# Router logits of the second expert layer taken from the state-space block's products, and the front of both expert layers put in another order

## The chip, the cores and the metric

The kernel runs on 1 core of a Trainium2 chip. The metric is device time in microseconds (us) of that core. Before the change three runs took 2043.24, 2030.67 and 2032.51 us, median 2032.51. TensorE is PE in the profile, VectorE is DVE, ScalarE is ACT, GpSimd is POOL; SP issues most DMAs.

## The reference, cut to what matters

Four blocks with residual sums work on 4 sequences of 1024 tokens of width 256: attention, an expert layer, a state-space block (mamba), and the same expert layer again with the same weights.

```python
x = x + attention(layernorm(x))
x = x + ffn(layernorm(x))
x = x + mamba(layernorm(x))        # its own residual adds the normed x once more
x = x + ffn(layernorm(x))

def ffn(x):                        # 4096 tokens, 4 experts, 1 taken per token
    logits = x @ Wr + br
    top_w, top_idx = top_k(softmax(logits), 1)
    h = silu(x @ Wg[e]) * (x @ Wu[e])        # 1024 wide
    return (h @ Wd[e])[top_idx] * top_w

def mamba(x):                      # returns x + ...
    z, xBC, dt = x @ w_in          # 512, 768 and 8 columns
    # convolution over 4 taps, chunked state-space product, gate by silu(z)
    y = y * rsqrt(mean(y * y) + eps) * norm_w
    return x + y @ w_out           # 512 to 256 columns
```

## The kernel before, in words

Tokens lie in 32 tiles of 128 rows, held on chip in `X` (shown as `x_res`). The four blocks run one after the other; between two of them all engines meet. Each engine runs its own list of instructions in written order and waits at semaphores.

**An expert layer** (`routed_ffn`, names `g_...`, `F["turn"]` 0 or 1) has a front and a loop of 35 slots. A slot is 128 tokens of one expert. The front makes the list of tokens for each slot:

- SP issues the loads of gate and up weights `w_gu` (8 DMAs of 1 MB, L1141), then the store of the last quarter of `X` to DRAM (`save_rows`, L106, 1 MB), on one queue.
- PE turns all 32 tiles (`turn_group`, L1476, 8 groups), ACT copies them out (L1425), PE multiplies them by the router's weights in two halves (`route`, L1490), ACT copies the logits (L1431), PE turns them back (L1499), DVE scales and shifts them (`scores`, L1206 and L1211).
- DVE finds the best expert of each token (L1219 to L1227), ranks tokens with two PE products, and works out each token's place (L1231 to L1251). Then it waits for the store (`saved`), since the marks that it writes next (L1254 on) lie where `X` was. It makes the token list `token_i` (L1274).
- POOL gathers the rows of the first slots (L1374). DVE normalises a slot's rows (`stats` L1299, `center` L1308), PE turns them (L1538), and DVE splits them into a rounded part and its remainder (`take`, L1313 and L1315).
- Weights are split in the same way, in 8 pieces of 128x2048: ACT rounds (`raise_high`, L1419), DVE subtracts (`lower`, L1183, written back over `w_gu`). The first slot's products (`first_up`, L1555) use the rounded weights first; their last part waits for all 8 remainders.
- Behind the pieces DVE works out the weights of the tokens (`weights`, L1278 to L1286). PE sorts them by slot with 32 products (`find(1, ...)`, L1524), and only after that goes on to the second slot (L1578).

The written order decides where the 8 subtractions stand: two ahead of each half of the scores (4), two behind the token list, two behind the first `take`.

**Mamba** (names `m_...`) runs for each of the 4 sequences a stage of convolutions (6 groups of 128 channels; `taps`, L1810 and L1811, three DVE operations of 128x1024 each) and then a loop over 8 tiles. `sizes` (L2184) multiplies each tile by the last 8 columns of `w_in`; `step_sizes` (L1821) takes the result. `output` (L2297) is 12 products per tile with `w_out`, split like the other weights into `w_out_hi` and `w_out_lo` (`scale_out`, `split_out`: L1801, L1802, L1914, L1916). `last` (L1905) adds the result to `X`. In the first stage POOL masks the decays (L1991).

## Time and profile before

| | us |
|---|---|
| median of three runs | 2032.51 (2030.67 to 2043.24) |
| the profiled execution's own time | 2058.66 |
| its span, first to last instruction | 2057.0 |
| attention | 0 to 795 |
| front of the first expert layer | 795 to 865 |
| its slots | 865 to 1204 |
| mamba | 1204 to 1654 |
| front of the second expert layer | 1654 to 1721 |
| its slots | 1721 to 2057 |

PE is busy 88% of the span, DVE 63%, ACT 43%, POOL 35%. A share of the span is an average over these six stages. In the two stages of slots PE is busy 327 of 336 to 339 us, in the two fronts 31 to 34 of 67 to 70 us, where DVE is busy 50 to 52 us. So a front is read from its own chain of waits and its timeline.

### The profile page before, as it was taken

How to read it: one execution, taken by the hardware profiler on the slowest of the kernel's cores; microseconds unless marked ns; L12 is line 12 of the kernel's file. 1: busy time of each engine (PE TensorE's matmuls, PEld its weight loads, DVE VectorE, ACT ScalarE, POOL GpSimd, SP SyncE). 2: the span in 40 equal slices, each digit the busy share in tenths (PEclk: the TensorE clock that was granted, in tenths of full speed). 3: DMA queues.
4: the chain of work that ended last, by engine and by line, in shares of the span. 5: the costliest groups of instructions: out<-in, count | busy, mean ns of one | idle time of the engine just before them, and what ended most of it. 6: DMA issues, size and time to landing. Idle time of an engine off the chain costs nothing. (4 is left out here: it accounts for less than half of the span.)

```text
span 2057.0 us, 32460 instructions
## 1 busy us (share of the span) xinstructions
PE 1803.7 (88%) x10701; PEld 1199.7 (58%) x10701; DVE 1290.4 (63%) x3148; ACT 877.0 (43%) x1799; POOL 724.4 (35%) x873
## 2 busy tenths in 40 slices
PE   5579989999989895499999968999899947999998
PEld 4133444444434333488888844848485736888886
DVE  4477677777676703755555528777777766555554
ACT  2146665665665743122222216474747451222221
POOL 2326355464463421123222213434343312232221
PEclk9668999999897957699999979999999978999999
DMA  5623353442544715267676642020202044676764
GB/s 157 211 80 114 113 150 108 127 129 93 152 132 143 224 53 193 94 241 258 240 257 243 240 143 83 1 103 1 103 1 103 1 186 184 239 260 238 259 244 173
DMA packets 103472, 312.39 MB, mean 152 GB/s; under 512 B 23304, under 2 KB 54796, under 8 KB 93200
## 3 DMA queue, kind: packets, MB, share of 16 engines
q1 hardware_dynamic: 84304, 257.06, 35.6%
q0 software_dynamic: 15936, 50.35, 8.1%
q10 hardware_dynamic: 3072, 2.90, 0.5%
q8 instruction: 93, 1.52, 0.3%
q14 instruction: 67, 0.55, 0.1%
HBM read 245.12 MB, written 53.87 MB: 145 GB/s over the span
## 5 line engine op out<-in xcount | busy, mean ns | idle before, releaser
L774 ACT ACTIVATE a_probs<-a_ps_e 128x512 f32<-128x512 f32 (+3 forms) x768 | 336.0, 491 | 183.3 <-PE a_ps_e L949 180.1
L511 DVE CUSTOM_DVE_ANT_0 a_ps_m<-a_ps_m,a_causal 128x512 f32<-128x512 f32 (+3 forms) x512 | 238.3, 517 | 84.1 <-PE a_ps_m L936 83.3
L1460 ACT CAST hidden_high<-g_ps_h 128x512 fp32r<-128x512 f32 x140 | 75.2, 590 | 398.8 <-PE g_ps_h L1605 398.8
L515 DVE TENSOR_REDUCE a_peak<-a_ps_m 128x1 f32<-128x512 f32 x256 | 164.1, 683 | 101.2 <-PE a_ps_m L936 99.9
L966 PE MATMUL a_ps_a<-a_probs,a_vals 128*32 128x256 f32 (+2 forms) x2560 | 216.8, 415 | 1.2 <-ACT a_probs L774 0.6
L949 PE MATMUL a_ps_e<-a_q_st,a_k_st 64*128 64x512 f32 (+3 forms) x768 | 189.6, 487 | 29.3 <-ACT a_probs L774 19.8
L653 POOL TENSOR_SCALAR_AFFINE_SELECT a_probs<-a_probs 128x256 f32<-128x256 f32 x256 | 104.5, 410 | 288.8 <-ACT a_probs L774 287.4
L936 PE MATMUL a_ps_m<-a_k_st,a_q_st 64*128 64x512 f32 (+3 forms) x768 | 157.0, 408 | 49.5 <-DMA a_k_st<-a_scr_k 23.0
L949 PEld LDWEIGHTS a_ps_e<-a_q_st,a_k_st 64*128 64x128 f32 x768 | 80.1, 204 | 199.2 <-ACT a_probs L774 137.7
L111 POOL TENSOR_TENSOR g_xe_rs<-g_xe_ve,table 128x1 f32<-128x1 f32 x70 | 39.4, 563 | 441.3 <-DVE g_xe_ve L1301 441.3
L1593 PE MATMUL g_ps_y<-g_w_d,hidden_high 128*128 128x512 f32 x560 | 144.2, 400 | 5.9 <-DVE x_res L1337 5.9
L1455 ACT ACTIVATE x_res<-g_ps_g 128x1024 f32<-128x1024 f32 x70 | 71.9, 1028 | 171.4 <-PE g_ps_g L1578 117.4
L936 PEld LDWEIGHTS a_ps_m<-a_k_st,a_q_st 64*128 64x128 f32 x768 | 86.3, 211 | 84.9 <-issue 36.7
L1321 DVE TENSOR_TENSOR x_res<-x_res,g_ps_u 128x1024 f32<-128x1024 f32 x70 | 85.5, 1222 | 69.2 <-PE g_ps_u L1578 69.2
L1593 PEld LDWEIGHTS g_ps_y<-g_w_d,hidden_high 128*128 128x128 f32 x560 | 106.2, 190 | 32.0 <-issue 6.3
L1328 DVE TENSOR_TENSOR hidden_less<-g_ps_h,hidden_high 128x512 fp32r<-128x512 f32 x140 | 90.2, 686 | 47.5 <-ACT hidden_high L1460 47.4
L1374 POOL DMA_INDIRECT x_res<-g_x_rows,g_token_i x70 | 76.0, 1086 | 93.5 <-DVE g_token_i L1274 73.1
L1313 DVE CAST g_xe_hi<-g_ps_x 128x256 fp32r<-128x256 f32 x70 | 29.8, 425 | 120.8 <-PE g_ps_x L1538 120.7
L966 PEld LDWEIGHTS a_ps_a<-a_probs,a_vals 128*32 128x32 f32 x2560 | 53.5, 114 | 81.3 <-issue 55.5
L1578 PE MATMUL g_ps_g<-g_w_hi,g_xe_hi 128*128 x272 | 91.6, 418 | 0.3 <-DVE g_xe_hi L1313 0.3
L2004 POOL TENSOR_TENSOR m_y<-m_y,m_z_act 128x512 f32<-128x512 f32 x32 | 40.7, 1272 | 135.0 <-DVE m_y L1894 119.3
L1578 PE MATMUL g_ps_u<-g_w_gu,g_xe_hi 128*128 x272 | 85.7, 396 | 0.0
(316 smaller groups left out, 3907.3 us busy)
## 6 DMA issues: line engine op xcount, KB each, us to landing
g_w_d<-down_rows SPq DMA_DIRECT2D x70, 2048.0 KB, 7.8
a_q_st<-a_scr_q POOLq DMA_DIRECT2D x32, 512.0 KB, 4.4
a_k_st<-a_scr_k POOLq DMA_DIRECT2D x32, 512.0 KB, 5.5
m_spread_acs<-m_acs_rows SPq DMA_DIRECT2D x8, 2048.0 KB, 10.0
a_scr_q<-a_high SPq DMA_DIRECT2D x34, 256.0 KB
a_scr_k<-a_high SPq DMA_DIRECT2D x32, 256.0 KB
a_swapped<-a_raw SPq DMA_DIRECT2D x64, 128.0 KB, 2.0
g_x_rows<-x_res SPq DMA_DIRECT2D x8, 1024.0 KB, 12.5
```

The lines of the kernel that those rows point to most:

```text
L511: nc.vector.tensor_tensor_reduce(ps_m[:, bank, 0:w], ps_m[:, bank, 0:w], causal[:, 512 - w:], 1.0, MASKED, ALU.add, ALU.max, peak[:, p % 2 ...
L515: nc.vector.tensor_reduce(peak[:, p % 2, r, i, c:c + 1], ps_m[:, bank, 0:w], AX, ALU.max).then_inc(chunk_max, 1)
L653: nc.gpsimd.affine_select(tile, tile, [[0, 2], [1, P]], ALU.is_ge, 0.0, base=0, channel_multiplier=-1).then_inc(masked, 1)
L774: nc.scalar.activation(probs[:, N % RING, r, q0:], ps_e[:, (2 * N + r) % HEAD_BANKS, q0:], ACT.Exp, scale=DH ** -0.5).then_inc(exp_done, 1)
L936: nc.tensor.matmul(banks[r][:, 0:w], q_st[rows(r), p % BUFS, i * P:(i + 1) * P], k_st[rows(r), p % BUFS, 512 * c:512 * c + w], start=True, ...
L949: nc.tensor.matmul(ps_e[:, (2 * N + r) % HEAD_BANKS, q0:], k_st[rows(r), p % BUFS, j * P:(j + 1) * P], q_st[rows(r), p % BUFS, 512 * c + q ...
L966: last = nc.tensor.matmul(ps_a[32 * u:32 * u + 32, some], vals[:, b % 2, j, 17 * h:17 * h + 32], probs[:, (U * CORE + 2 * m + u // 2) % RI ...
L1321: nc.vector.tensor_tensor(hid, gate, ps_u[:].rearrange("p b f -> p (b f)"), ALU.mult).then_inc(hid_ready, 1)
L1328: nc.vector.tensor_tensor(hid_lo[:, some], ps_h[:, c], hid_hi[:, some].bitcast(F32), ALU.subtract).then_inc(ht_lo, 1)
L1374: nc.gpsimd.indirect_dma_start(out=xe[:, j % XE], out_offset=None, in_=x_rows, in_offset=bass.IndirectOffsetOnAxis(ap=token_i[:, j:j + 1], ...
L1578: last = nc.tensor.matmul(ps[:, c], x[:, d * P:(d + 1) * P], w[:, :, d].rearrange("p a f -> p (a f)"), start=(n == d == 0), stop=(n == len ...
L1593: nc.tensor.matmul(ps_y[:], hid_hi[:, f * P:(f + 1) * P], w[:, f], start=(f == 0), stop=False, skip_group_check=True)
```

## The change

In mamba, 4 router columns go beside what is multiplied anyway. `sizes` gets a table `w_sizes` of 12 columns (8 step sizes, 4 router columns), loaded by two small DMAs ahead of `w_in`. Once, at the start, PE turns `w_out` (`turn_w_out`), ACT copies it, and PE multiplies it by the router's weights (`route_weights`); DVE scales and splits the 16 values of each row (`routed_columns`) into 4 new columns of `w_out_hi` and `w_out_lo`. So each product of `output` is 260 columns wide in place of 256. DVE adds the parts up in `raw_logits`: `growth` and `add_means` for each sequence, one operation in `step_sizes`, and one of 128x4 in each `last`.

In the second expert layer turning the tiles, the router's products and turning the logits back are left out; DVE reads `raw_logits` (`ready_scores`). In the first layer PE and ACT do all logits before ACT rounds the first piece of the weights. In both layers ACT rounds the 8 pieces in a row; DVE's subtractions ahead of the scores are gone. POOL does pieces 0 and 1, behind the roots of the variances and ahead of its wait for the token list; DVE does two pieces behind the token list and four behind the first `take`.

```diff
+        BY_POOL = (0, 1)
+        BY_DVE = [n for n in range(len(PIECES)) if n not in BY_POOL]
...
-            sp.wait_ge(turned_ps, HALVES)
+            if F["turn"] == 0:
+                sp.wait_ge(turned_ps, HALVES)
...
-            for n in range(2):
-                lower(n)
-            scores(0)
-            for n in range(2, 4):
-                lower(n)
-            scores(1)
+            def ready_scores():
+
+                step(nc.vector.tensor_tensor(logits[:], C["raw_logits"][:], all_experts(rstd[:]), ALU.mult))
+                step(nc.vector.tensor_tensor(logits[:], logits[:], shift[:], ALU.add))
+
+            if F["turn"] == 0:
+                scores(0)
+                scores(1)
+            else:
+                ready_scores()
...
-            for n in range(4, 6):
+            for n in BY_DVE[:2]:
                 lower(n)
             stats(0)
             center(0)
             take(0)
-            for n in range(6, len(PIECES)):
+            for n in BY_DVE[2:]:
                 lower(n)
             stats(1)
...
+            for n in BY_POOL:
+                e, d = PIECES[n]
+                pool.wait_ge(hi_ready, n + 1)
+                nc.gpsimd.tensor_tensor(columns(e)[:, d].bitcast(F32R), columns(e)[:, d], w_hi[:, e, d].bitcast(F32),
+                                        ALU.subtract).then_inc(lo_ready, 1)
             pool.wait_ge(saved, 16 * BATCH)
             pool.wait_ge(token_ready, 1)
...
-            for g in range(4):
-                turned(g)
-            raise_high(0)
-            take_logits(0)
-            turned(4)
-            raise_high(1)
-            turned(5)
-            raise_high(2)
-            turned(6)
-            turned(7)
-            raise_high(3)
-            take_logits(1)
-            for n in range(4, len(PIECES)):
+            if F["turn"] == 0:
+                for g in range(4):
+                    turned(g)
+                take_logits(0)
+                for g in range(4, 8):
+                    turned(g)
+                take_logits(1)
+            for n in range(len(PIECES)):
                 raise_high(n)
...
-            for g in range(2):
-                turn_group(g)
-            sum_weights()
-            for g in range(2, 4):
-                turn_group(g)
-            route(0)
-            turn_group(4)
-            turn_logits(0)
-            for g in range(5, 8):
-                turn_group(g)
-            route(1)
-            turn_logits(1)
+            if F["turn"] == 0:
+                for g in range(4):
+                    turn_group(g)
+                sum_weights()
+                route(0)
+                turn_group(4)
+                turn_logits(0)
+                for g in range(5, 8):
+                    turn_group(g)
+                route(1)
+                turn_logits(1)
+            else:
+                sum_weights()
...
+        SIZES = MHEADS + EXPERTS
+        sizes_ps = ps_r[:, 1, 0:T * SIZES].rearrange("p (t h) -> p t h", h=SIZES)
...
+        w_out_hi = sb("w_out_hi", [P, ZT, D + EXPERTS], F32R)
+        w_out_lo = sb("w_out_lo", [P, ZT, D + EXPERTS], F32R)
...
+                sp.dma_start(w_sizes[:, :, 0:MHEADS], M["w_in"][:, INNER + CONV:].rearrange("(t p) e -> p t e", p=P)
+                             ).then_inc(w_in_ready, 16)
+                sp.dma_start(w_sizes[:, :, MHEADS:SIZES], M["Wr"].rearrange("(t p) e -> p t e", p=P)
+                             ).then_inc(w_in_ready, 16)
             sp.dma_start(w_in[:], M["w_in"].rearrange("(t p) e -> p t e", p=P)).then_inc(w_in_ready, 16)
...
+                sp.dma_start(w_r[:], M["Wr"].rearrange("(t p) e -> p t e", p=P)).then_inc(route_in, 16)
...
+                    dve.wait_ge(w_turned, DT)
...
+                nc.vector.tensor_tensor(raw[:, b * T:(b + 1) * T], sizes_ps[:, :, MHEADS:SIZES],
+                                        grown[:].unsqueeze(2).to_broadcast([P, T, EXPERTS]), ALU.mult
+                                        ).then_inc(parts_used, 1)
+
+            def growth(b):
+
+                some = slice(b * T, (b + 1) * T)
+                if b >= 1:
+                    dve.wait_ge(rstd_ready, b + 1)
+                    dve.wait_ge(parts_used, b)
+                step(nc.vector.tensor_tensor(grown[:], var_eps[:, some], rstd[:, some], ALU.mult))
+                step(nc.vector.tensor_scalar(grown[:], grown[:], 1.0, None, ALU.add))
+
+            def add_means(b):
+
+                some, per_tile = slice(b * T, (b + 1) * T), [P, T, EXPERTS]
+                dve.wait_ge(parts_used, b + 1)
+                step(nc.vector.tensor_tensor(by_mean[:], mean_var[:, some, 0].unsqueeze(2).to_broadcast(per_tile),
+                                             w_sums[:].unsqueeze(1).to_broadcast(per_tile), ALU.mult))
+                step(nc.vector.tensor_tensor(raw[:, some], raw[:, some], by_mean[:], ALU.add))
+
+            def routed_columns():
+
+                dve.wait_ge(routed_ps, 1)
+                dve.wait_ge(loaded, 16 * 5)
+                step(nc.vector.tensor_tensor(routed[:], ps_z[:, 0, 0:ZT * EXPERTS].rearrange("p (k e) -> p k e", e=EXPERTS),
+                                             norm_w[:].unsqueeze(2).to_broadcast([P, ZT, EXPERTS]), ALU.mult))
+                nc.vector.tensor_copy(w_sums[:], ps_z[:, 0, ZT * EXPERTS:(ZT + 1) * EXPERTS]).then_inc(routed_used, 1)
+                dve.wait_ge(routed_used, 1)
+                step(nc.vector.tensor_copy(w_out_hi[:, :, D:D + EXPERTS], routed[:]))
+                step(nc.vector.tensor_tensor(w_out_lo[:, :, D:D + EXPERTS], routed[:], w_out_hi[:, :, D:D + EXPERTS],
+                                             ALU.subtract))
...
+                step(nc.vector.scalar_tensor_tensor(raw[:, N], ps_z[:, 0, D:D + EXPERTS], rms[:], raw[:, N], ALU.mult,
+                                                    ALU.add), wait=False)
                 nc.vector.scalar_tensor_tensor(X[:, N], ps_z[:, 0, 0:D], rms[:], X[:, N], ALU.mult, ALU.add
...
+            growth(0)
             step_sizes(0)
             for b in range(BATCH):
                 more_sizes(b)
...
                     last(b * T - 1)
                 for n in range(1, CT):
                     taps(b, n)
+                    if b == 0 and n == 2:
+                        routed_columns()
+                    if n == 4:
+                        add_means(b)
                     if b == 0 and n <= ZT:
...
+                        growth(b + 1)
                         step_sizes(b + 1)
...
+                if b == 0:
+                    for d in range(DT):
+                        act.wait_ge(w_turned, d + 1)
+                        nc.scalar.copy(y[:, d].rearrange("p h f -> p (h f)"), (ps_s, ps_z)[d][:, 0]).then_inc(w_turned_sb, 1)
...
+                    pe.wait_ge(w_in_ready, 16 * 3)
                 for t in tiles:
                     for d in range(DT):
-                        one = nc.tensor.matmul(sizes_ps[:, t * MHEADS:(t + 1) * MHEADS], xn_t[:, d, t * P:(t + 1) * P],
-                                               w_in[:, d, INNER + CONV:], start=(d == 0), stop=(d == DT - 1))
+                        one = nc.tensor.matmul(sizes_ps[:, t], xn_t[:, d, t * P:(t + 1) * P],
+                                               w_sizes[:, d], start=(d == 0), stop=(d == DT - 1))
...
+                    pe.wait_ge(parts_used, b + 1)
+                if t == 2 and b == 0:
+                    pe.wait_ge(routed_used, 1)
...
-                        one = nc.tensor.matmul(ps_z[:, 0, 0:D], part[:, k * P:(k + 1) * P], w[:, k],
+                        one = nc.tensor.matmul(ps_z[:, 0, 0:D + EXPERTS], part[:, k * P:(k + 1) * P], w[:, k],
                                                start=(n == k == 0), stop=(n == 2 and k == ZT - 1))
                 one.then_inc(out_ps, 1)
+
+            def turn_w_out():
+
+                pe.wait_ge(loaded, 16 * 5)
+                for d in range(DT):
+                    for k in range(ZT):
+                        one = nc.tensor.transpose((ps_s, ps_z)[d][:, 0, k * P:(k + 1) * P], w_out[:, k, d * P:(d + 1) * P],
+                                                  ident)
+                    one.then_inc(w_turned, 1)
+
+            def route_weights():
+
+                pe.wait_ge(w_turned_sb, DT)
+                pe.wait_ge(route_in, 16)
+                for k in range(ZT):
+                    for d in range(DT):
+                        at = y[:, d].rearrange("p h f -> p (h f)")
+                        nc.tensor.matmul(ps_z[:, 0, k * EXPERTS:(k + 1) * EXPERTS], at[:, k * P:(k + 1) * P], w_r[:, d],
+                                         start=(d == 0), stop=(d == DT - 1))
+                for d in range(DT):
+                    one = nc.tensor.matmul(ps_z[:, 0, ZT * EXPERTS:(ZT + 1) * EXPERTS], ones[:], w_r[:, d], start=(d == 0),
+                                           stop=(d == DT - 1))
+                one.then_inc(routed_ps, 1)
...
+                        if b == 0:
+                            turn_w_out()
                         if b >= 1:
...
+                    if n == 1 and b == 0:
+                        route_weights()
```

The first place is DVE's list in the first layer, from the shift of the logits to the best expert. `g_w_gu` is the weights, `g_w_hi` their rounded part. Before:

```order
L1201 TENSOR_TENSOR g_shift<-g_b_r,g_shift 128x128
L1183 TENSOR_TENSOR g_w_gu<-g_w_gu,g_w_hi 128x2048 x2
L1206 TENSOR_TENSOR g_logits<-g_ps_x,g_rstd 128x64
L1211 TENSOR_TENSOR g_logits<-g_logits,g_shift 128x64
L1183 TENSOR_TENSOR g_w_gu<-g_w_gu,g_w_hi 128x2048 x2
L1206 TENSOR_TENSOR g_logits<-g_ps_y,g_rstd 128x64
L1211 TENSOR_TENSOR g_logits<-g_logits,g_shift 128x64
L1219 TENSOR_REDUCE g_best<-g_logits 128x32
```

Now:

```order
L1204 TENSOR_TENSOR g_shift<-g_b_r,g_shift 128x128
L1209 TENSOR_TENSOR g_logits<-g_ps_x,g_rstd 128x64
L1214 TENSOR_TENSOR g_logits<-g_logits,g_shift 128x64
L1209 TENSOR_TENSOR g_logits<-g_ps_y,g_rstd 128x64
L1214 TENSOR_TENSOR g_logits<-g_logits,g_shift 128x64
L1226 TENSOR_REDUCE g_best<-g_logits 128x32
```

The four subtractions have left this place. The second place is DVE's list behind the token list, in either layer. Before:

```order
L1274 CAST g_token_i<-g_token 128x35
L1183 TENSOR_TENSOR g_w_gu<-g_w_gu,g_w_hi 128x2048 x2
L1299 BN_STATS g_xe_stats<-x_res 128x6
L1308 TENSOR_SCALAR x_res<-x_res,g_xe_mv,g_xe_rs 128x256
...
L1315 TENSOR_TENSOR g_xe_lo<-g_ps_x,g_xe_hi 128x256
L1183 TENSOR_TENSOR g_w_gu<-g_w_gu,g_w_hi 128x2048 x2
L1299 BN_STATS g_xe_stats<-x_res 128x6
```

Now:

```order
L1281 CAST g_token_i<-g_token 128x35
L1186 TENSOR_TENSOR g_w_gu<-g_w_gu,g_w_hi 128x2048 x2
L1306 BN_STATS g_xe_stats<-x_res 128x6
...
L1315 TENSOR_SCALAR x_res<-x_res,g_xe_mv,g_xe_rs 128x256
...
L1322 TENSOR_TENSOR g_xe_lo<-g_ps_x,g_xe_hi 128x256
L1186 TENSOR_TENSOR g_w_gu<-g_w_gu,g_w_hi 128x2048 x4
L1306 BN_STATS g_xe_stats<-x_res 128x6
```

Behind the first `take` four subtractions stand where two stood. The third place is POOL's list in the front of either layer, now:

```order
L111 TENSOR_TENSOR g_rstd<-g_var_eps,table 128x24
L111 TENSOR_TENSOR g_rstd<-g_var_eps,table 128x8
L1405 TENSOR_TENSOR g_w_gu<-g_w_gu,g_w_hi 128x2048 x2
L1381 DMA x_res<-g_x_rows,g_token_i 128x256 x3
L111 TENSOR_TENSOR g_xe_rs<-g_xe_ve,table 128x1 x3
```

The two subtractions are new on POOL; before, the gathers followed the roots.

## Rows read from the trace of the kernel before

**Rows 1.** Second front: its us, busy us of PE, PEld, DVE, ACT, POOL; granted clock

```profile
1654.00:1721.00 67.00, 31.41 (x210) 21.56 (x210) 49.72 (x131) 25.87 (x23) 12.01 (x7) 0.69 0.56 211
```

**Rows 2.** Chain that ended last, second layer's front: start us, us, what

```profile
1679.88 0.30 DVE g_best L1219
...
1687.90 1.34 DVE x_res L1254
...
1707.38 4.40 DVE g_w_gu L1183 x2
...
1718.10 1.71 PE g_ps_y L1524 x32
```

**Rows 3.** Timeline, second layer's front: start us, us, instruction, [idle before <-releaser]

```profile
1663.64 0.29 DVE L1201 TENSOR_TENSOR g_shift<-g_b_r,g_shift 128x128 f32<-128x128 f32 x1
1663.76 2.29 SPq L106 DMA_DIRECT2D g_x_rows<-x_res  x1
1664.17 1.90 ACT L1419 CAST g_w_hi<-g_w_gu 128x2048 fp32r<-128x2048 f32 x1 [2.21 <-DMA g_w_gu<-L_ffn_Wu]
```

**Rows 4.** The DRAM copy of `X` (`g_x_rows`), all its DMAs: issue to landing, us

```profile
DMA to landing us min/median/max: 2.2/2.9/19.7
```

**Rows 5.** Timeline, first layer's front

```profile
807.44 1.53 PE L1476 MATMUL g_ps_g<-table,x_res 128*128 128x128 f32 x8
815.35 1.03 ACT L1425 COPY g_later<-g_ps_u 128x1024 f32<-128x1024 f32 x1
816.43 3.64 PE L1490 MATMUL g_ps_h<-g_later,g_w_r 128*32 128x512 f32 x16 [2.53 <-ACT g_later L1425]
820.14 0.59 ACT L1431 COPY g_later<-g_ps_h 128x512 f32<-128x512 f32 x1 [1.96 <-PE g_ps_h L1490]
823.58 0.22 DVE L1225 TENSOR_TENSOR g_hot<-g_hot,g_taken 128x32 f32<-128x32 f32 x1
830.46 1.33 DVE L1254 TENSOR_TENSOR x_res<-g_slot,table 128x1120 bf16<-128x1120 f32 x1
```

**Rows 6.** POOL's 128x512 and 128x256 operations of mamba: duration ns min/median/max

```profile
L2004 POOL TENSOR_TENSOR m_y<-m_y,m_z_act x32: 1265/1271/1291, 1282.5 to 1648.3; 128x512 f32<-128x512 f32 x32
L1985 POOL TENSOR_TENSOR x_res<-x_res,m_xn x32: 719/731/827, 1215.3 to 1550.0; 128x256 f32<-128x256 f32 x32
```

**Rows 7.** Timeline in attention: the same DVE operation alone, and beside POOL

```profile
39.22 0.69 DVE L541 TENSOR_TENSOR a_raw<-a_raw,a_swapped 128x512 f32<-128x512 f32 x1
40.90 1.34 POOL L631 TENSOR_TENSOR a_low<-a_raw,a_high 128x512 f32<-128x512 f32 x1 [16.39 <-ACT a_high L758]
41.15 1.64 DVE L541 TENSOR_TENSOR a_raw<-a_raw,a_swapped 128x512 f32<-128x512 f32 x1
```

**Rows 8.** Timeline in mamba's first stage: POOL's masks, a DVE copy beside and after them

```profile
1243.20 11.65 POOL L1991 TENSOR_SCALAR_AFFINE_SELECT m_spread_acs<-m_spread_acs 128x1024 f32<-128x1024 f32 x8 [22.37 <-DMA m_spread_acs<-m_acs_rows]
1243.32 1.13 DVE L1914 CAST m_w_out_hi<-m_w_out 128x256 fp32r<-128x256 f32 x1
1268.98 0.30 DVE L1914 CAST m_w_out_hi<-m_w_out 128x256 fp32r<-128x256 f32 x1
```

**Rows 9.** PE, first layer and second: the sorting products, and the second slot's end

```profile
860.66 3.01 PE L1524 MATMUL g_ps_y<-x_res 128*128 128x105 bf16 x32 [3.77 <-DVE x_res L1286]
871.57 2.03 PE L1593 MATMUL g_ps_y<-g_w_d,hidden_high 128*128 128x512 f32 x8
1726.83 2.03 PE L1593 MATMUL g_ps_y<-g_w_d,hidden_high 128*128 128x512 f32 x8
```

**Rows 10.** Mamba: its first convolutions by stretch, and the small DMAs of its start

```profile
1235.00:1262.00 27.00, 23.39 (x52) 9.92 (x51) 26.31 (x32) 21.96 (x37) 11.65 (x8) 0.94 0.38 157
q10 hardware_dynamic: 1712, 0.02, 7.3%
```

**Rows 11.** Timeline in mamba: 8 narrow products, and a small DVE operation

```profile
1335.19 1.01 PE L2184 MATMUL m_ps_r<-m_w_in,m_xn_t 128*128 128x8 f32 x8
1341.02 0.21 DVE L1821 TENSOR_TENSOR m_dtv<-m_ps_r,m_dt_bias 128x64 f32<-128x64 f32 x1
```

More of the change, by code:

```diff
@@ L2397, in program @@
         C["stats"] = ctx.enter_context(nc.sbuf_tensor("row_statistics", [P, NT, 6], F32))
+        C["kept"] = ctx
         C["sems"] = Semaphores(nc, ctx)
@@ L2433, in phase_mamba @@
 def phase_mamba(nc, X, C, I, out):
-    mamba(nc, X, C, {k: I["L0_attn_b_" + k]
-                     for k in ("w_in", "conv_w", "conv_b", "dt_bias", "A_log", "D", "norm_w", "w_out")})
+    M = {k: I["L0_attn_b_" + k] for k in ("w_in", "conv_w", "conv_b", "dt_bias", "A_log", "D", "norm_w", "w_out")}
+    M["Wr"] = I["L0_ffn_Wr"]
+    C["raw_logits"] = C["kept"].enter_context(nc.sbuf_tensor("raw_logits", [P, NT, EXPERTS], F32))
+    mamba(nc, X, C, M)
 PHASES = [phase_attention, phase_ffn("g1_"), phase_mamba, phase_ffn("g2_")]
```

21 lines of the change are left out of this document (13 added, 8 removed).

## Prediction

> **What bounds the kernel now.** I read the table of stages first. The loops of slots and the tile loops of mamba belong to PE, and the change adds only narrow columns there. The two fronts are not bound by a busy engine: in the second one PE works 31.4 of 67 us, at 0.69 of full clock [rows 1]. So I took the chain of waits of that front [rows 2]. It runs through DVE: the best expert at 1679.88, the marks at 1687.90 (8.0 us of small operations later), two weight remainders at 1707.38 behind the first `take`, then the weights of the tokens, then PE's sorting products at 1718.10, and from there PE never waits long again. Everything that delays DVE in this chain delays the end by as much. Third I read both fronts' timelines [rows 3, 5], for what runs beside the chain and would take its place.
>
> **Second layer's front: the logits come early, the store does not.** The chain can start behind the shift at 1663.64 + 0.29 = 1663.9 [rows 3], with two operations of about 0.3 us for `ready_scores`. The best expert would be looked for at about 1664.6 where it was 1679.88: 15.3 us earlier. Without disturbance the marks could start at 1672.6. But DVE waits there for the store of `X`. It is issued at 1663.76 [rows 3] behind 8 MB of weights on the same queue, and its landing takes up to 19.7 us, the maximum of its group, which is this one by its place in the queue [rows 4]: 1683.5. Nothing ahead of it in SP's list has changed. Before, the wait was covered (1687.90). Now it ends last, and the marks start at 1683.5: **-4.4 us**, not -15.3.
>
> Behind the first `take` DVE now has four remainders in place of two. Two cost 4.40 us [rows 2]; the weights of the tokens, the sorting and the second slot wait for DVE: **+4.4 us**. The four remainders that went from ahead of the scores had cost nothing there, since DVE only waited for logits. The two behind the token list still fit into the wait for the gather, as before. POOL's two are done long before the token list.
>
> PE's clock: the first slot's high products end 4.4 us earlier against the remainders, so PE has a hole there. With the clock at half level the way from the sorting products to the second slot's end took 871.57 - 860.66 = 10.9 us in the first layer, at the full level 1726.83 - 1718.10 = 8.7 us in the second [rows 2, 9]. Whether the hole costs these 2.2 us I can't tell; I take half, **+1.1 us**, ends 0 and 2.2. The second front sums to +1.1.
>
> **First layer's front: earlier logits, then POOL in the way.** PE turns group 4 at 807.44 as before [rows 5]. Then ACT's four copies of 1.03 us follow PE's turns without a rounding between them: I get them done at 813.8 where it was 816.38, so the second half's products start at 813.9 where it was 816.43. The logits are 2.5 us earlier.
>
> Now ACT rounds only behind its last copy of logits: 820.14 + 0.59 - 2.5 = 818.2, so piece 0 is ready at 820.1 and POOL starts to subtract. No POOL operation of 128x2048 is in the trace. 128x256 takes 731 ns and 128x512 takes 1271 [rows 6]; the line through both gives 4.5 us, mere proportion 5.1. I take 4.5, as the two sizes show a fixed part. Two of them fill 820.1 to 829.4, just while DVE works on its list of small operations.
>
> What that does to DVE: in attention a DVE operation with two on-chip inputs takes 0.69 us alone and 1.64 us when started at 41.15 beside a POOL operation that ends at 42.24; it begins to work as POOL ends [rows 7]. In mamba the same DVE copy takes 1.13 us beside POOL's masks and 0.30 after them [rows 8]. So DVE's list stops for POOL. The list has such an operation every 0.5 us. One (the subtraction of the best logit) stops until 824.6, then the next (the second expert's, 823.58 before) until 829.4. From that one to the marks it is 830.46 - 823.58 = 6.9 us [rows 5]: the marks start at 836.3, **+5.8 us** in place of -2.5. If POOL lets DVE in more often, as the masks do (they take 1.46 us each, and a DVE operation waits 0.8), DVE gets about eight operations in while POOL works: a delay of 7.7 us instead of 8.3, +5.2. With 5.1 us per subtraction it is +7.0. The trace thus gives 5.2 to 7.0; 5.8 stands, nearest to the attention rows, which are the same kind of operation.
>
> The Trainium skill, page SBUF — State Buffer, section "SBUF: two separate sides", says that VectorE and GpSimd share a port pair which one of them holds for a whole instruction. By that alone the mamba masks would have held the copy until each ended; rows 8 show shorter waits, so I don't carry it past the attention rows. By it the sum would be the same 5.8 to 7.0.
>
> In the second layer the same stop falls to 1666.1 (piece 0: 1664.17 + 1.90 [rows 3]) to 1675.4. The list then ends at about 1681.5, still ahead of the store. It costs nothing there; the cover is 2.0 us, and beyond it every us counts.
>
> The two more remainders behind `take` cost +4.4 here too, for the same reason; the store, issued as early in this front as in the other, is no limit at 836. ACT's eight roundings of 1.90 us end at 833.4; the next two remainders are DVE's behind the token list, later than that. First front: 5.8 + 4.4 = **+10.2 us**.
>
> **Mamba: only additions.** A small DVE operation takes 0.21 us [rows 11], about 0.23 with its wait. DVE is busy 26.3 of 27 us in the convolutions [rows 10], so there all counts.
> - Start: PE waits for the load of `w_in`, and 512 small packets now go ahead of it. 1712 small packets took 7.3% of 16 engines in 16 us, 11 ns each [rows 10]: 512 x 11 / 16 = 0.4 us. The shortest landing in [rows 4], 2.2 us, is the upper end. I take 0.4, since the queue runs full there and only the packets count.
> - First sequence: 8 turns ahead of the second channel group, 1.0 us by the 8 products of 1.01 us [rows 11]; the 10 router products (1.3 us) and ACT's two copies hide behind DVE's convolutions. `routed_columns`: 4 operations, 0.9. POOL's masks also stop them, but they only take the place of others that were stopped. `add_means`: 0.5. Together 2.4.
> - Three later sequences: `growth` 0.5 ahead of `step_sizes`, 0.15 for the logits in `last`, `add_means` 0.5: 1.15 x 3 = 3.5. The extra operation in `step_sizes` hides while ACT takes an exponential.
> - Tile loops: 384 products 4 columns longer at 2.4 GHz, 1.7 ns each, 0.6 us. The 32 operations of 128x4 (up to 0.15 each, 4.8) find DVE waiting for PE in nearly every tile; I take 0.3.
>
> Sum **+7.2 us**. Ends: 4 (half of DVE's work in the convolutions hidden, nothing in the tiles) and 14 (start 2.2, every small operation exposed, and 1 us for the gate products that now wait for `routed_columns`).
>
> **Sum.** 10.2 + 7.2 + 1.1 = +18.5 us. The profiled execution took 2058.66 us and lies 26 us above the median of the runs, 2032.51; I take the difference over unchanged. 2032.5 + 18.5 = 2051 us, 0.9% more. What a measurement here can tell from no change is about 1%, 20 us.
>
> **Rivals.**
> 1. *POOL does not stop the list* (not slower). Its subtractions of 128x2048 would let DVE's small operations through; then the first list is 2.5 us earlier, not 5.8 later. It decides in one place, DVE's operations of 820 to 829. For it: nothing of this size is in the trace, and most list operations need the port only briefly. Against: rows 7 and 8. 18.5 - 8.3 = +10.2: 2043 us, within 1%. With mamba at its low end too, 2040. Chance 0.2.
> 2. *Mamba pays in full* (slower by over 1%). Every tile's operation shows, and the clock costs 2.2: 10.2 + 14 + 2.2 = +26: 2059 us. For it: mamba's engines wait on each other in short turns, so a delay is rarely swallowed. Against: DVE has idle time in every tile. Chance 0.25.
> 3. *The store isn't the limit* in the second layer (it lands by 1673): the lists start up to 11 us earlier than forecast, but POOL's stop then shows, with marks at 1681.5: 18.5 - 2 = +16.5, 2049 us. Only with rival 1 as well would it be 1672.6: 18.5 - 8.3 - 10.9 = -1, 2032 us. Against: 9 MB on one queue ahead of its end. Chance 0.05.
> 4. *The remainders behind `take` don't count*, since something else ends last there: 18.5 - 8.8 = +10, 2042 us. Against: the chain goes through them. Chance 0.05.
>
> The forecast keeps 0.45, with 2045 to 2058 as its own range. The range over all cases: 2038 to 2061. Slower by over 1% (above 2053): rival 2 with 0.22, and 0.14 of the forecast's own: 0.36. Faster by over 1%: nothing in the trace gives it; 0.03. Within 1%: 0.61.
>
> **What would show it.** In the profile after: the marks of the second layer start as the store lands, with DVE idle for some us ahead of them (right), or earlier (rival 3). POOL's two subtractions in the first layer last 4.5 to 5.1 us each, and DVE's small operations beside them 1 to 5 us instead of 0.2 (right), or unchanged (rival 1). Four remainders of 8.9 us behind `take` in both layers, and the sorting products that much later. Mamba longer by about 7 us, most of it in the convolutions. The slots' loops should not change at all; if they do, the forecast is wrong for a reason that isn't in it.

## Result, and the profile after

The changed kernel takes 2050.03 us (median of 20 runs, 2032.97 to 2069.61), the kernel before, timed beside it, 2039.07 (median of 20, 2027.8 to 2046.84). The ratio is 1.0046 with a 95% interval of 1.0027 to 1.0065: +9.4 us (5.5 to 13.3): slower, but by less than the bound of 1%. The ratio leaves out two executions of the changed kernel in a slower state (2065.47 and 2069.61 us), so it gives less than the 11.0 us between the two medians. The forecast was 2051 us, +18.5 over a median of three runs that lay 6.6 us under the later median. The absolute time is met by luck, since this low start made up for most of what the forecast difference was too large. The forecast is judged here by its terms, since one of them was badly off and others made up for it.

Spans of single executions can't be set against each other as wholes. The first layer's front begins at 796.04 us in the profile of before and at 777.04 in that of the change, though nothing ahead of it differs; in the profiles of this study it begins between 765 and 796. So I compare stages. A front is counted from its first memset on DVE to the second slot's first product. The second front:

```profile
1642.75 0.11 DVE L1168 MEMSET g_w_r<- 128x64 f32 x1 [0.58 <-PEq L1645]
1652.10 0.29 DVE L1218 TENSOR_TENSOR g_logits<-raw_logits,g_rstd 128x128 f32<-128x128 f32 x1
1652.75 0.29 DVE L1226 TENSOR_REDUCE g_best<-g_logits 128x32 f32<-128x128 f32 x1
...
1654.13 4.51 DVE L1233 TENSOR_TENSOR g_taken<-g_hot,g_taken 128x32 f32<-128x32 f32 x1
1658.67 4.45 DVE L1232 TENSOR_TENSOR g_hot<-g_hot,g_taken 128x32 f32<-128x32 f32 x1
...
1669.08 0.18 DVE L1258 CAST g_taken<-g_slot_i 128x32 f32<-128x32 int32 x1
1670.25 1.33 DVE L1261 TENSOR_TENSOR x_res<-g_slot,table 128x1120 bf16<-128x1120 f32 x1 [0.99 <-DMA g_x_rows<-x_res]
```

These are DVE's timeline rows. The best expert stands 10.0 us behind the memset, where it stood 25.3 behind it [rows 2]. The marks (L1261) stand only 27.5 us behind it, 5.8 earlier than before, since they wait for the store. The chain of waits (start us, us, what) goes through it and then through four remainders in place of two:

```profile
1651.51 18.65 DMA g_x_rows<-x_res
1670.25 1.34 DVE x_res L1261
...
1689.73 8.80 DVE g_w_gu L1186 x4
...
1702.23 2.57 DVE x_res L1293 x2
1704.85 3.01 PE g_ps_y L1532 x32
```

Last, PE's side of the same place, from its timeline. The second half of the first slot's products waits 3.5 us for the remainders, and the sorting products run at the half level of the clock (3.01 us; before 1.71 [rows 2]), the full level coming back in the second slot:

```profile
1698.67 1.17 PE L1563 MATMUL g_ps_g<-g_w_gu,g_xe_hi 128*128 x4 [3.52 <-DVE g_w_gu L1186]
1704.85 3.01 PE L1532 MATMUL g_ps_y<-x_res 128*128 128x105 bf16 x32 [3.62 <-DVE x_res L1293]
1709.66 1.02 PE L1586 MATMUL g_ps_g<-g_w_hi,g_xe_hi 128*128 x2
```

By stretch (columns as in [rows 1]), PE is busy 19.06 us where it was 31.41, at clock 0.57, and DVE 53.41 instead of 49.72:

```profile
1643.00:1710.00 67.00, 19.06 (x107) 15.00 (x108) 53.41 (x126) 17.52 (x12) 20.97 (x9) 0.57 0.55 211
```

The rise of DVE is not work: its two operations of 4.51 and 4.45 us above take 0.2 us elsewhere, and for the rest of that time they stand beside POOL's subtractions.

In the first layer's front the answer to [rows 5] begins earlier than the forecast looked. PE, ACT and POOL, from their timelines:

```profile
781.38 0.60 PE L1490 MATMUL g_ps_y<-g_w_r,g_later 128*128 128x32 f32 x4 [0.20 <-DMA g_lanes<-const_lanes]
782.28 1.92 PE L1497 MATMUL g_ps_h<-g_later,g_w_r 128*32 128x512 f32 x16 [0.30 <-ACT g_later L1437]
...
788.77 1.01 ACT L1437 COPY g_later<-g_ps_u 128x1024 f32<-128x1024 f32 x1 [0.27 <-PE g_ps_u L1483]
...
789.83 1.92 PE L1497 MATMUL g_ps_h<-g_later,g_w_r 128*32 128x512 f32 x16 [1.10 <-ACT g_later L1437]
...
794.29 8.99 POOL L1405 TENSOR_TENSOR g_w_gu<-g_w_gu,g_w_hi 128x2048 fp32r<-128x2048 f32 x2 [8.89 <-ACT g_w_hi L1431]
```

And DVE's list beside POOL's two subtractions, which take 4.5 us each:

```profile
793.74 0.29 DVE L1226 TENSOR_REDUCE g_best<-g_logits 128x32 f32<-128x128 f32 x1
794.39 4.49 DVE L1229 TENSOR_SCALAR g_hot<-g_logits 128x128 f32<-128x128 f32 x1
798.92 4.41 DVE L1230 COPY g_taken<-g_hot 128x32 f32<-128x32 f32 x1
803.36 0.22 DVE L1232 TENSOR_TENSOR g_hot<-g_hot,g_taken 128x32 f32<-128x32 f32 x1
...
810.24 1.33 DVE L1261 TENSOR_TENSOR x_res<-g_slot,table 128x1120 bf16<-128x1120 f32 x1
```

Two operations of 0.2 us take 4.49 and 4.41 us, and then the list goes on at its pace. The best expert comes 16.7 us behind the memset (26.4 before), the marks 33.2 behind it (34.4 before).

The stages of all profiles, in us, worked out from such rows. "Best" and "marks" are us behind the front's memset; "sequences" is mamba from the first convolution product of its first sequence to the second front's memset:

| kernel | first front: best, marks, length | sequences | second front: best, marks, length |
|---|---|---|---|
| before | 26.4, 34.4, 69.4 | 427.6 | 25.3, 33.3, 66.5 |
| the change | 16.7, 33.2, 72.6 | 429.3 | 10.0, 27.5, 66.9 |
| first_front_only | 16.7, 33.2, 72.6 | 424.2 | 26.4, 34.4, 69.4 |
| mamba_only | 25.1, 33.2, 67.5 | 428.7 | 24.7, 32.7, 66.5 |
| none_by_pool | 18.2, 28.6, 71.8 | 428.3 | 10.0, 27.7, 70.9 |
| fill_the_wait | 19.0, 31.3, 69.7 | 430.6 | 10.0, 27.4, 62.4 |
| pool_quarters | 19.2, 35.0, 73.4 | 430.1 | 10.0, 27.6, 66.3 |
| sums_back | 21.5, 38.0, 76.3 | 430.5 | 10.0, 27.7, 66.5 |
| store_first | 26.4, 34.4, 67.7 | 430.8 | 10.0, 18.0, 61.8 |
| tile_ops_x6 | 25.1, 33.1, 67.2 | 438.4 | 25.4, 33.4, 66.6 |
| sums_moved | 24.9, 32.9, 67.1 | 430.1 | 10.0, 18.0, 61.8 |
| mamba_again | 25.3, 33.3, 67.9 | 429.7 | 25.0, 33.0, 67.4 |
| means_x6 | 26.4, 34.4, 69.4 | 440.9 | 25.5, 33.5, 68.6 |
| before_sums_moved | 25.0, 33.1, 67.1 | 427.0 | 24.3, 32.2, 65.5 |

It also shows how well a stage repeats. A first front in the old order takes 67.2 to 69.4 us (mean of six: 68.2), a second one 66.5 to 69.4 (mean of six: 67.5), mamba's unchanged sequences 424.2 to 427.6 (mean of three: 426.2). The two loops of slots, which the forecast named as a sign, don't tell the kernels apart: from the second slot's first product to mamba's first product 344.4 us before, 345.5 in the change and 342.7 to 345.8 in all; from the second layer's second slot to the end 335.8, 337.0 and 334.3 to 339.1.

### The profile page after: what moved, and what is told of

Its sections match the earlier page's. It is cut to its first block and busy times, and to the rows that moved or that the text cites. A ratio compares the mean times of both kernels' runs of the same rounds, so it can differ in the third digit from the quotient of the medians.

```text
span 2046.7 us, 32361 instructions
## 1 busy us (share of the span) xinstructions
PE 1769.9 (86%) x10625; PEld 1189.3 (58%) x10625; DVE 1304.6 (64%) x3198; ACT 868.5 (42%) x1791; POOL 742.0 (36%) x877
## 5 line engine op out<-in xcount | busy, mean ns | idle before, releaser
L949 PE MATMUL a_ps_e<-a_q_st,a_k_st 64*128 64x512 f32 (+3 forms) x768 | 185.4, 476 | 30.1 <-ACT a_probs L774 20.2
L966 PE MATMUL a_ps_a<-a_probs,a_vals 128*32 128x256 f32 (+2 forms) x2560 | 210.3, 404 | 0.0
L1601 PEld LDWEIGHTS g_ps_y<-g_w_d,hidden_high 128*128 128x128 f32 x560 | 107.0, 191 | 32.2 <-issue 6.3
```

Of the source, the lines that this page charges most:

```text
L949: nc.tensor.matmul(ps_e[:, (2 * N + r) % HEAD_BANKS, q0:], k_st[rows(r), p % BUFS, j * P:(j + 1) * P], q_st[rows(r), p % BUFS, 512 * c + q ...
L966: last = nc.tensor.matmul(ps_a[32 * u:32 * u + 32, some], vals[:, b % 2, j, 17 * h:17 * h + 32], probs[:, (U * CORE + 2 * m + u // 2) % RI ...
L1601: nc.tensor.matmul(ps_y[:], hid_hi[:, f * P:(f + 1) * P], w[:, f], start=(f == 0), stop=False, skip_group_check=True)
```

## Experiments

Each ratio is against the kernel before, timed beside it, with its 95% interval.

### The new first front alone

```diff
+        BY_POOL = (0, 1) if F["turn"] == 0 else ()
...
+            if F["turn"] == 0:
+                scores(0)
+                scores(1)
+            else:
 ...  (the order of before)
```

> The kernel before with the new order of the first layer's front alone (logits ahead of the roundings, two remainders on POOL, two behind the token list, four behind `take`); mamba and the second front as before. Theory from the profile of the change: the front grows from 69.4 us (its memset to the second slot's first product) to about 72.6, because POOL stops DVE's list for 8.4 us but the logits come 9 to 10 us earlier; the whole kernel +3 us over before (0.15%). Rival, the forecast's own sum: the logits come only 2.5 us earlier and the lead in the profile of the change was luck of the clock: front 79.6, whole kernel +10 us. Mamba stays at 445 us and the second front at 66.5 in both.

Ratio 1.0058 (1.0027 to 1.0089). The front took 72.6 us, as in the change, with best and marks at the same places to 0.1 us. So the early logits were no luck of one execution, and the forecast's 79.6 is refuted. Against the old order's mean of 68.2 the new order costs 4.4 us. The time says 11.8 us (5.5 to 18.1), more than the stage; see "Open" below.

### The changed mamba alone, twice

```diff
-                ready_scores()
 ...  (turns, routes and remainders in both fronts as before)
```

> The changed mamba, which also sums the second layer's logits, with both fronts as before: they turn and route for themselves, and mamba's logits are left unused. Theory from the stages of the profile of the change: mamba 447.6 us where it was 444.8, whole kernel +3 us. Rival, the forecast: mamba +7.2, 452 us, whole kernel +7; rival 2 of the forecast: 459 us, +14. Fronts 69.4 and 66.5 us in all.

> `mamba_only` once more, unchanged, since its stages (mamba 4 us longer) and its times (11.6 us more, 7 to 16) disagree. If the stages are right, 4 us over before; if the times are, 12; the other comparisons (the change, `fill_the_wait`, `store_first`) leave 4 to 6 for mamba once their fronts are taken off, so 6 is expected, and mamba's four sequences at 429 us.

Ratios 1.0057 (1.0036 to 1.0079) and 1.0063 (1.0035 to 1.0092). The sequences took 428.7 and 429.7 us. The stages support +3 to +4, the times +12. The repetition did not bring the two together, and my guess of 6 was wrong.

### No remainder on POOL

```diff
-        BY_POOL = (0, 1)
+        BY_POOL = ()
```

> The changed kernel, POOL takes no remainder; DVE has two behind the token list and six behind the first `take`. Theory (POOL's two subtractions stop DVE's list for 8.4 us in both fronts, and each remainder behind `take` costs 2.2 us): in the first layer the marks start 27.5 us after the memset, where the store lands, in place of 33.2, and two more remainders cost 4.4: front 71.4 us where the change has 72.6. In the second layer the list ends 8 to 9 us earlier, the marks still wait for the store and don't move, the remainders cost 4.4: front 71.4 where the change has 67.0. Whole kernel 3 us over the change, 12 over before. Rival: DVE's long operations there are not POOL's doing: marks at 33 us as in the change, first front 77, whole kernel 9 over the change. Rival: the store is not what the marks of the second layer wait for: they start 18 to 19 us after the memset, and that front is 62 us.

Ratio 1.0078 (1.0049 to 1.0107). The same two list operations in the second front, and the wait for the store (DVE's timeline):

```profile
1647.91 0.23 DVE L1229 TENSOR_SCALAR g_hot<-g_logits 128x128 f32<-128x128 f32 x1
1648.17 0.19 DVE L1230 COPY g_taken<-g_hot 128x32 f32<-128x32 f32 x1
...
1664.98 1.33 DVE L1261 TENSOR_TENSOR x_res<-g_slot,table 128x1120 bf16<-128x1120 f32 x1 [9.75 <-DMA g_x_rows<-x_res]
```

0.23 and 0.19 us: the 4.4 us were POOL's doing. The list ends 9.75 us before the store lands, and the marks stay where they were. Both fronts came out within 0.5 us of what was expected, 71.8 and 70.9: two more remainders behind `take` cost 4 us in the second layer, and in the first POOL's absence gives back about as much as they cost, the marks, at 28.6, now waiting for the store there too.

### Remainders in the wait for the store

```diff
-        BY_POOL = (0, 1)
+        BY_POOL = () if F["turn"] == 0 else ()
+        EARLY = 2 if F["turn"] == 0 else 4
...
+            for n in BY_DVE[:EARLY]:
+                lower(n)
             dve.wait_ge(saved, 16 * BATCH)
```

> The changed kernel without POOL's remainders; DVE takes four of them in the second layer (two in the first) between the end of its list and the wait for the store, then two behind the token list, and what is left (two, and four) behind the first `take`. Theory: second layer: marks where they are in the change, 27.5 us after the memset, and two remainders fewer behind `take`: front 67.0 less 3.5 to 4.4, 63 us. First layer: list ends 24.8 us after the memset, two remainders, marks at 29.2 in place of 33.2, the rest as in the change: front 68.6. Whole kernel 8 us under the change, within 2 us of before. Rival: the remainders behind `take` aren't on the path, since something else ends last there: second front stays at 67.

Ratio 1.0010 (0.9989 to 1.0032). In the second front four remainders fit ahead of the store with 0.46 us to spare (DVE's timeline):

```profile
1650.71 8.90 DVE L1187 TENSOR_TENSOR g_w_gu<-g_w_gu,g_w_hi 128x2048 fp32r<-128x2048 f32 x4
1660.07 1.33 DVE L1264 TENSOR_TENSOR x_res<-g_slot,table 128x1120 bf16<-128x1120 f32 x1 [0.46 <-DMA g_x_rows<-x_res]
```

The front takes 62.4 us, 4.5 less than the change (expected: 63). So the remainders behind `take` are on the path, 2.2 us each, and rival 4 is refuted. The first front took 69.7 instead of 68.6, because its logits came 2.3 us later than in the change (the reason stands with the next experiment).

### POOL's subtraction in quarters

```diff
+                for q in range(4):
+                    part = slice(q * 512, (q + 1) * 512)
+                    some = nc.gpsimd.tensor_tensor(...[:, d, part] ..., ALU.subtract)
```

> The changed kernel, with each of POOL's two subtractions cut into four instructions of 128x512, some 1.27 us each where the whole one takes 4.5. Theory (a DVE operation that needs what POOL holds starts when the POOL instruction ends, and gets in between two of them): DVE's list loses about 1 us per POOL instruction, 7 to 9 such stops of 1.2 us in place of two of 4.4, about as long in all or 1 to 2 us less, since one DVE operation gets through at every gap: marks of the first layer 31.5 to 33.5 us after the memset. Rival (POOL keeps its hold over instructions that follow each other without a gap): the same two stops of 4 to 5 us, marks at 33.5 or later. Rival 2 (DVE is stopped by the memory traffic, not by instructions): every operation beside POOL is slower by the same factor.

One execution, 2044.12 us. POOL's eight instructions and DVE's list (timelines):

```profile
793.39 9.86 POOL L1407 TENSOR_TENSOR g_w_gu<-g_w_gu,g_w_hi 128x512 fp32r<-128x512 f32 x8 [11.35 <-ACT g_w_hi L1434]
```

```profile
793.50 1.25 DVE L1229 TENSOR_SCALAR g_hot<-g_logits 128x128 f32<-128x128 f32 x1
794.78 1.15 DVE L1230 COPY g_taken<-g_hot 128x32 f32<-128x32 f32 x1
795.97 1.22 DVE L1232 TENSOR_TENSOR g_hot<-g_hot,g_taken 128x32 f32<-128x32 f32 x1
...
802.13 1.17 DVE L1233 TENSOR_TENSOR g_taken<-g_hot,g_taken 128x32 f32<-128x32 f32 x1
803.34 0.23 DVE L1234 CAST g_hot_b<-g_hot 128x128 bf16<-128x128 f32 x1
```

Eight POOL instructions let exactly eight DVE operations through, each 1.15 to 1.25 us long, and the ninth is back at 0.23. DVE is stopped instruction by instruction, not slowed. From the best expert to the marks it took 15.9 us, against 16.5 with two whole subtractions and 8.0 without POOL. The marks at 35.0 lie outside what was expected only since the logits came 2.5 us later here: PE's first turned groups ran at the half level of the clock in this execution (1.94 us per eight products; 1.06 in the change). The Trainium skill, page SBUF — State Buffer, section "Who interferes with whom", calls it an exclusive lock on a shared port pair; by that rule each stop should last as long as POOL's instruction, and these rows agree (1.2 us beside 1.23, 4.4 beside 4.5).

### `sum_weights` back, and moved alone

```diff
-                for g in range(4):
+                for g in range(2):
                     turn_group(g)
                 sum_weights()
+                for g in range(2, 4):
+                    turn_group(g)
```

> The changed kernel with the first layer's `sum_weights` back where it was on PE, behind two turned groups; everything else as in the change. Theory: it waits there for the small loads, in the kernel before until 3.8 us after the memset, and that wait was 2.1 to 2.6 us of the lead of 9.7 that the logits won: the best expert now comes at 18.5 to 19.5 us after the memset in place of 16.7, and the marks 2 us later, 35. Rival (the forecast's view that PE's turns are where they were and only ACT's copies gain): no difference, 16.7.

One execution, 2038.49 us. The best expert comes at 21.5 us, 4.8 later than in the change: more than expected, and the rival is refuted. PE's timeline shows two parts of it, the stop and then `route` at the half level of the clock:

```profile
769.00 0.60 PE L1490 MATMUL g_ps_y<-g_w_r,g_later 128*128 128x32 f32 x4 [1.95 <-DMA g_lanes<-const_lanes]
...
773.03 3.64 PE L1497 MATMUL g_ps_h<-g_later,g_w_r 128*32 128x512 f32 x16 [1.10 <-ACT g_later L1437]
```

`route` starts 7.9 us behind the memset (5.2 in the change) and takes 1.7 us longer. The kernel before with only this line moved, in both layers:

> The kernel before with `sum_weights` behind four turned groups on PE in both fronts, and nothing else of the change. Theory: PE's stop of 1.9 us for the small loads goes and `route` keeps the full clock, in both layers: the best expert 1 to 4 us earlier, each front 1 to 2 us shorter (66.5 to 69.4 before), whole kernel 2 to 4 us under before (0.998 to 0.999). Rival (the remainders or the arrival of the weights bound it): no change at all.

Ratio 1.0003 (0.9980 to 1.0025). The stop went and the first `route` took 1.92 us, but the first front's best expert only moved to 25.0 us: in the old order ACT's roundings still stand between its copies, the second `route` waits 2.29 us for them, and DVE's fourth remainder ends only at 23.8. The fronts are 1 and 2 us shorter than the old order's means; the time shows nothing.

### The store ahead of the weights

```diff
+            if F["turn"] == 1:
+                save_rows(sp, X, C, F["turn"], BATCH - 1)
             for e in range(EXPERTS):
                 for k, w in enumerate(("Wg", "Wu")):
...
-            save_rows(sp, X, C, F["turn"], BATCH - 1)
+            if F["turn"] == 0:
+                save_rows(sp, X, C, F["turn"], BATCH - 1)
```

(first front in the old order, POOL without remainders, two behind the second list and six behind `take`)

> First front in the order of the kernel before; second front as in the change, but the store of X is issued ahead of the 8 MB of weights, POOL takes no remainder, and DVE takes two behind the list and six behind the first `take`. Theory (the store was the only thing that held the marks in `none_by_pool`): they start where the list ends, 18.2 us after the memset in place of 27.7, and the whole front shrinks by 9.5, from 70.9 to 61.4 us. First front 67.5 to 69.4. Mamba by its stages 4 us over before. Whole kernel 2 us under before, if mamba costs 4; 5 over, if it costs the 11.6 that the times of `mamba_only` gave. Rival (the weights come later for it, and the front is bound by their roundings): front at 64 us or more.

Ratio 0.9992 (0.9969 to 1.0014). The list runs into the marks without a wait, 18.0 us behind the memset, and the front takes 61.8 us (expected: 61.4):

```profile
1653.77 0.17 DVE L1263 CAST g_taken<-g_slot_i 128x32 f32<-128x32 int32 x1
1653.97 1.33 DVE L1266 TENSOR_TENSOR x_res<-g_slot,table 128x1120 bf16<-128x1120 f32 x1
```

The store lands 5.5 us after its issue in place of 18.65. It was the only thing that held the marks. The ratio of the change, 1.0046, lies above this interval: this version beats the change. It does not beat the kernel before.

> `store_first` with one more move: in the first layer's front `sum_weights` stands behind four turned groups on PE instead of two, as in the change. Theory: PE no longer stops 1.9 us for the small loads there and `route` runs at the full level of the clock (1.92 us in place of 3.6); ACT's copies, the roundings and DVE's remainders come 1 to 3 us earlier: first front 65 to 66.5 us in place of 67.7. Rest as `store_first`: second front 61.8, mamba's four sequences 430.8. Whole kernel 2 us under `store_first`, 3 to 4 under before (0.998), which is about what can be told from no change. Rival (DVE's remainders hold the front, whose roundings hang on the arrival of the weights and not on PE): first front unchanged at 67.5.

Ratio 1.0021 (0.9994 to 1.0047). The first front took 67.1 us, only 0.6 less: DVE's fourth remainder ended 24.4 us behind the memset and the best expert followed at 24.9. The rival was nearly right.

### Mamba's small operations, multiplied

```diff
+                for i in range(5):       # in `last`, once per tile
+                    step(nc.vector.tensor_scalar(spare[:, N % 2, i], ps_z[:, 0, D:D + EXPERTS], rms[:], None, ALU.mult),
```

> `mamba_only` with five more operations of 128x4 per tile beside the one that the change adds in `last` (same inputs, into a tile that nobody reads), 160 in all. If the one operation hides in DVE's idle time, as the forecast had it (0.3 us for all 32), most of five hide too: mamba's four sequences 428.8 us as in `mamba_only`, at most 5 more. If it is exposed, 160 x 0.15 to 0.2 us = 24 to 32 us more, and the one operation per tile costs 5 to 6 of the mamba's cost.

Ratio 1.0077 (1.0049 to 1.0106). 160 operations of 0.21 us added 9.6 us to `mamba_only`'s sequences, 60 ns each, so about 30% shows. It falls between the two expectations. If the single operation of the change shows in the same share, its 32 cost 1.9 us; it may be less, as the first one finds the idle time free.

```diff
+                for _ in range(10):      # in `add_means`, once per sequence
+                    step(nc.vector.tensor_tensor(by_mean[:], ..., ALU.mult))
```

> `mamba_only` with ten more operations in `add_means` of each sequence (the product of the means, 128x32, each waiting for the one before), 40 in all, in the convolutions. Forecast's view (DVE is busy there without a break, so all of it shows): 40 x 0.23 = 9 us more, 2.3 in each sequence: mamba's four sequences 438 us. Rival (the convolutions have slack behind the fifth channel group that takes in what the change adds): under 2 us more.

Ratio 1.0089 (1.0057 to 1.0121). The sequences took 440.9 us, 12.2 more than in `mamba_only` and 11.2 more than in `mamba_again`, for 40 operations that take 0.19 us (0.22 with their wait, 9 us in all). Over the four sequences the small operations show in full, and the rival is refuted. By sequence it is uneven: against `mamba_again` 3.7, 2.3, 4.0 and 1.1 us, where 2.2 each were put in.

## Why the prediction was right, and where not

**The bound was read rightly.** The chain through DVE, the store as the next limit and the remainders behind `take` all acted as forecast. The table gives the first front +4.4 us against the mean of old-order fronts (+3.2 between the two profiles), the second front -0.9 against such a mean (66.6 in three profiles; +0.4 between the two), and mamba's sequences +3.6 (nine changed ones average 429.8; +1.7 between the two), with 0.7 for mamba's start (from its first product to the first of `sizes`, 11.6 us in the mean of the nine, 10.9 in the three unchanged). That makes 7.8 us by the means, within the measured 5.5 to 13.3; the forecast's 18.5 is not. The 10.7 us too many lie in the first front (5.8), in mamba (2.9) and in the second front (2.0).

**Second front** (forecast +1.1; measured +0.4 between the two profiles, -0.9 by the means). Best expert 15.3 us earlier, as forecast to 0.1. The marks came 5.8 us earlier, not 4.4: the store landed 18.65 us after its issue, where I had taken 19.7 [rows 4], and was issued 0.4 us earlier behind the memset. That is no chance of one execution: in the five kernels with the second front's new order and the store last it landed after 18.3 to 18.8 us, in the seven with the old order after 19.2 to 20.4. Why is not shown. Remainders +4.4, as forecast. The clock took 1.8 us between the two profiles, where I had taken 1.1: from the sorting products to the second slot's first product 4.8 us instead of 3.1. But this stretch took 3.1 to 4.8 us in six second fronts of the old order too (mean 3.9), and 4.1 to 4.8 in seven of the new one (mean 4.5), so only about 0.6 can be put down to the change. `none_by_pool` and `store_first` show POOL's stop was covered here; of the forecast cover of 2.0 us 1 was left. Rival 3 (the store isn't the limit) is refuted.

**First front: the step that failed** is "PE turns group 4 at 807.44 as before". The forecast kept PE's times and let only ACT gain, so the logits were to come 2.5 us earlier. The change also moves `sum_weights` behind two more groups, and in the profile of before PE stopped for the small loads just there:

```profile
799.86 0.60 PE L1483 MATMUL g_ps_y<-g_w_r,g_later 128*128 128x32 f32 x4 [1.93 <-DMA g_lanes<-const_lanes]
```

I had the row and left out what the moved instruction waits for. The logits came 9.7 us earlier. `sums_back` puts 4.8 of it on this one line (the stop, and `route` at the half level after it). ACT's roundings, which no longer stand between its copies, make 2.8: the second `route` starts 17.6 us behind the memset in `sums_back`, 20.4 before. That is the gain that I had forecast as 2.5. Another 1.7 is this `route` at the full level, 1.92 us instead of 3.64. POOL's stop was right: forecast 8.3 us, measured 8.5 between best and marks (I let two subtractions of 4.5 us fill 9.3; they took 8.99). So the marks came 1.2 us earlier than in that profile, and even with the old fronts that ran at full clock (33.2), where +5.8 had been forecast; of the forecast's 10.2 the two remainders, +4.4, are left. Rival 1 (POOL does not stop the list) gave 2043 us, closer to the true difference, by a mechanism that isn't there.

**Mamba** (forecast +7.2; stages +4). By sequence, means of the changed kernels less the unchanged: 1.4 in the first (forecast 2.4), then 0.7, 0.5 and 0.9 (forecast 1.15 each, and 0.9 for all tile loops); start 0.7 (0.4). `means_x6` shows that operations in the convolutions cost in full over the four sequences. So 1.0 us too many was counted in the first sequence, perhaps the turns of `w_out` on PE (1.0), which DVE's convolutions may cover, and 1.3 or more in the three later ones; neither was run alone, and the first sequence of an unchanged mamba varies by 1.4 us itself (111.6 to 113.0). The tiles' operation (0.3) may cost up to 1.9. Rival 2, mamba in full at 14, is refuted by every profile's stages, though not by every time.

**Open.** `mamba_only` cost 12 us in its times, twice, and `first_front_only` 12; their stages give 4 each. The changed kernel holds both and costs 9; `store_first` holds that mamba and costs nothing, with a second front that is 5.7 us shorter. Part of this is which execution was profiled: that of `mamba_only` took 2036.36 us, the second shortest of its twelve (median 2045.69), that of `mamba_again` 2040.81 (median 2045.47). The one of `first_front_only`, 2051.21, is at its median of 2050.50. It is 17.5 us longer than the one of `before_sums_moved` (2033.74, median 2035.04), of which only 5.6 lie in the first front; 7.6 lie in attention, 3.9 in the second front and 3.3 in the last slots, none of which the edit of `first_front_only` touches (the second front of `before_sums_moved` has its `sum_weights` moved), and its sequences are 2.8 shorter. Longer executions of one kernel mostly have a lower mean granted clock (`mamba_again`: 0.93 in its shortest of 2032.64, 0.91 in its second longest of 2060.79). Why two of the kernels should have more of them is not shown, so the 8 us stay unexplained.

## What to carry to other kernels

When an instruction moves in a list, write down what it waited for in its old place: its neighbours inherit the wait's end, and here one small product's stop for a load, with the slower products behind it, was half of a 10 us lead. A chain that is shortened stops at the next arrival, so look first for the transfer queued behind large ones; issuing the store ahead of 8 MB of weights made the front 9.1 us shorter (70.9 to 61.8), and only then did DVE's work bound the front. Work put on POOL is free only while DVE waits, whatever DVE's own list looks like.

## What the runs showed of the hardware

- A POOL subtraction of 128x2048 takes 4.5 us, and two small DVE operations with a single input (a comparison of 128x128 with a constant, a copy of 128x32) are stopped for its whole length, 4.49 and 4.41 us, like those with two inputs (4.51 and 4.45 us in the second front). Eight of 128x512, 1.23 us each, stop eight DVE operations of 1.15 to 1.25 us. That single-input operations wait too was new to me. The Trainium skill, page VectorE: DVE Perf Modes, section "Mode 2×_2P — use both read ports for one tensor", says that a float32 `tensor_scalar` or copy within SBUF reads its one tensor through both ports; these rows agree. The Trainium skill, page GPSIMD Engine Reference, section "3.1 Elementwise — side-by-side cycle accounting", gives 4497 ns for an addition with 2048 float32 elements; the two subtractions here, 8.99 us, agree.
- PE's clock: in five profiles PE stopped 1.89 to 1.96 us for the small loads in the first front, and in four of them the next `route` ran at the half level (1.2 GHz), 3.55 to 3.64 us; in the fifth (`mamba_again`) it took 1.92, the full level (2.4 GHz). In all nine where that stop was 0.61 us or less it took 1.92. That the stop lowered the clock is not shown by this: all five with the long stop began the front at the full level (1.06 us per eight products), and seven of the nine began it at the half level (1.94), where PE comes to the stop later and finds the load nearly landed. Only the change and `first_front_only` began at the full level and stopped 0.20 us or less. The level is not settled by the kernel alone: `mamba_only` and `mamba_again` are the same kernel, and one began this front at the half level, the other at the full one.
- The store of `X` (1 MB) in the second front lands 5.5 us after its issue ahead of the weights (`store_first`, `sums_moved`: 5.51 and 5.55) and 18.3 to 20.4 us behind them (18.65 in the change), on the same queue.
